# Gathering 64-number node rows instead of 128-number projected rows in a two-layer graph network's message loop

## The reference, cut to what matters

```python
h = jnp.maximum(_layernorm(x, axis=-1), 0.0)          # node rows, 64 numbers
msg_input = jnp.concatenate([h[src], edge_sh, edge_radial], axis=-1)   # 64 + 9 + 8
m = jax.nn.silu(msg_input @ W1 + b1)                  # 81 -> 128
m = jax.nn.silu(m @ W2 + b2)                          # 128 -> 128
messages = m @ W3 + b3                                # 128 -> 64
aggregated = jax.ops.segment_sum(messages, dst, num_segments=6250)
update_input = jnp.concatenate([h, aggregated], axis=-1)
gate = jax.nn.sigmoid(update_input @ G + gb)
u = jax.nn.silu(_layernorm(update_input @ U1 + ub1, ln1_g, ln1_b))
update = _layernorm(u @ U2 + ub2, ln2_g, ln2_b)
out = x + h + gate * update
```

## Time and profile before

| what | value |
|---|---|
| three runs | 3262.56, 3270.5 and 3275.14 us, median 3270.5 |
| span of the profiled execution | 3264.2 us |
| mean granted TensorE clock, as a share of 2.4 GHz | 0.940 |
| busy share PE, DVE, ACT, POOL | 87%, 45%, 47%, 48% |
| data moved | 391.13 MB read, 240.52 MB written |

### The profile page before, as it was taken

One profiled execution on the slowest core, in us unless ns is written; L12 is line 12 of the kernel. 1 busy time (PEld: TensorE's weight loads), 2 busy tenths in 40 slices (PEclk: granted clock), 3 DMA queues, 4 the chain that ended last, 5 costly groups with the idle time before them and its releaser, 6 DMA issues.

```text
span 3264.2 us, 59125 instructions
## 1 busy us (share of the span) xinstructions
PE 2847.1 (87%) x18211; PEld 2118.1 (65%) x18211; DVE 1468.1 (45%) x2016; ACT 1543.7 (47%) x2600; POOL 1565.9 (48%) x1663
## 2 busy tenths in 40 slices
PE   3599999859999969899989888988888989998894
PEld 2477777759989955566555555555555655655563
DVE  7999999863445543222222222222222222222227
ACT  2588888723332214444444444444444444444456
POOL 4000000000000017777777777777777777777765
PEclk8799999959999979999999999999999999999995
DMA  3133333429979966776776777777676777767752
GB/s 127 62 155 157 143 152 157 168 79 370 364 314 352 347 196 181 189 195 189 191 192 189 189 189 194 189 194 189 190 193 189 191 189 190 195 191 191 192 155 68
DMA packets 355148, 632.41 MB, mean 194 GB/s; under 512 B 42566, under 2 KB 251017, under 8 KB 336092
## 3 DMA queue, kind: packets, MB, share of 16 engines
q1 hardware_dynamic: 299973, 519.99, 48.1%
q0 software_dynamic: 54128, 110.18, 15.0%
q10 hardware_dynamic: 1001, 1.66, 0.1%
HBM read 391.13 MB, written 240.52 MB: 194 GB/s over the span
## 4 chain that ended last, share of the span: by engine, by line
PE 37%; POOL 29%; issue 12%; DMA 12%; DVE 8%; ACT 1%; POOLq 0%; DVEq 0%; ACTq 0%
POOL arena L635 27%; PE ps L772 17%; DMA arena<-p_tab,m_idx 11%; PE ps L791 6%; PE ps L949 5%; PE ps L968 3%; DVE arena L1807 2%; PE ps L958 2%; PE ps L946 2%; DVE stageT L1783 2%; POOL arena L648 1%; PE ps L673 1%; PE ps L823 1%; PE ps L661 1%; POOL arena L576 0%
## 5 line engine op out<-in xcount | busy, mean ns | idle before, releaser
L635 POOL DMA_INDIRECT arena<-p_tab,m_idx x1563 | 1474.7, 944 | 1611.2 <-issue 1568.5
L2029 DVE TENSOR_TENSOR_SCAN arena<-arena,ps 128x512 f32<-128x512 f32 x391 | 500.4, 1280 | 1033.8 <-ACT ps L1280 1019.7
L949 PEld LDWEIGHTS ps<-ident,arena 128*128 128x128 f32 x3126 | 391.6, 197 | 517.6 <-DMA arena<-p_tab,m_idx 426.6
L968 PEld LDWEIGHTS ps<-w_fold,arena 128*128 128x128 f32 x3128 | 555.1, 198 | 202.8 <-issue 202.8
L1275 ACT ACTIVATE arena<-ps 128x512 f32<-128x512 f32 x391 | 233.5, 597 | 887.1 <-PE ps L949 884.1
L949 PE MATMUL ps<-ident,arena 128*128 128x128 f32 x3126 | 468.7, 295 | 203.0 <-DMA arena<-p_tab,m_idx 201.7
L968 PE MATMUL ps<-w_fold,arena 128*128 128x192 f32 x3128 | 593.7, 335 | 0.0
L772 PE MATMUL ps<-arena 128*128 128x195 bf16 (+1 forms) x4802 | 481.1, 248 | 31.9 <-DVE arena L1749 31.3
L772 PEld LDWEIGHTS ps<-arena 128*128 128x128 f16 x4802 | 416.5, 98 | 62.8 <-DVE arena L1749 31.5
L946 PE MATMUL ps<-arena,weights 17*128 17x512 f32 x782 | 440.9, 643 | 1.7 <-issue 1.7
L958 PE MATMUL ps<-arena,weights 128*128 128x512 f32 x782 | 427.5, 630 | 0.0
(11 more groups left out here) (257 smaller groups left out, 1637.8 us busy)
## 6 DMA issues: line engine op xcount, KB each, us to landing
arena<-count_d SPq DMA_DIRECT2D x98, 1568.0 KB, 8.6
scan_rows<-arena SPq DMA_DIRECT2D x391, 384.0 KB, 3.5
arena<-keep_d SPq DMA_DIRECT2D x391, 256.0 KB, 4.6
count_d<-arena SPq DMA_DIRECT2D x49, 1568.0 KB, 5.1
arena<-p_tab,m_idx POOLq DMA_INDIRECT x1563
arena<-attr_in SPq DMA_DIRECT2D x391, 34.0 KB
p_tab<-ends SPq DMA_DIRECT2D x12, 256.0 KB, 5.0
wide<-hT_d SPq DMA_DIRECT2D x1, 1617.0 KB
```

The costliest lines, as they stand in the source:

```text
L635: pool.indirect_dma_start(m_rows[:, k, t, :], None, p_tab, bass.IndirectOffsetOnAxis(ap=m_idx[:, k, t:t + 1].bitcast(U32), axis=0))\
L949: last = pe.matmul(x[:, t * P:(t + 1) * P], m_rows[:, k, t, :], ident[:, :], start=False, stop=(t == tiles_of - 1), skip_group_check=True)
L968: last = pe.matmul(m_back[h][:, t * ROW:(t + 1) * ROW], m_scan[:, k % SCAN_RING, e_at:e_at + P], w_fold[:, :], start=True, stop=True)
L2029: dve.tensor_tensor_scan(m_scan[:, k % SCAN_RING, :], m_mask[:, k, :], m_term[k % TERM_RING], before, ALU.mult, ALU.add).then_inc(e1.scan_ ...
```

## The change

**The table.** `p_tab` becomes `m_tab`, which holds the normalised relu'd rows themselves, 64 numbers per node. `multiply_table` and `use_table` go; `stage_table` writes the relu into `hbuf` and SP stores it from there. The turned rows for `hT_d` stay.

**The loop.** POOL gathers 256-byte rows into a ring of 12 slots (`LOOP` 12). PE turns the four tiles (`turn_rows`), ACT copies the turned 64 x 512 next to the 17 attribute rows in SBUF (`keep_turned`), and one product with all 81 rows of W1 follows (`hidden_in`, now one slot behind; W2's product two behind; `LAG` 4). b1 comes in with the first silu. `rows_back` multiplies by W3 alone (64 columns), ACT copies 256 columns in one instruction, and SP stores rows of 64 numbers, four edges next to each other per partition.

**The end.** The gathered 64-number rows are turned (`turn_agg`), copied by ACT (`copy_agg`) and multiplied on PE by the aggregate's rows of U1 and G (`agg_product`), and `add_h` reads that product from PSUM. Groups are six tiles, so there are nine. `turn_update`, `hidden_update` and `update_out` of a group now stand behind the first steps of the next one. `fold` keeps only b3's product.

**The last edges.** Eight more small DVE instructions turn an edge's number into its place in the new layout of `scan_rows`.

```diff
-LOOP = 8
+LOOP = 12
-ROW_RING = MASK_RING = LOOP
-ATTR_RING, TERM_RING, SCAN_RING, OUT_RING = 4, 4, 4, 4
-HID_RING = 2
-LAG = 3
+ROW_RING = LOOP
+MASK_RING = 6
+ATTR_RING, TERM_RING, SCAN_RING, OUT_RING = 4, 3, 4, 4
+HID_RING, BACK_RING = 2, 1
+LAG = 4
...
-END_GROUPS = [(0, 7), (7, 7), (14, 7), (21, 7), (28, 7), (35, 7), (42, 4), (46, 3)]
-GATES_AT = {1: (0, 2), 3: (2, 4), 5: (4, 6), 7: (6, 8)}
+END_GROUPS = [(0, 6), (6, 6), (12, 6), (18, 6), (24, 6), (30, 6), (36, 6), (42, 4), (46, 3)]
+GATES_AT = {1: (0, 2), 3: (2, 4), 5: (4, 6), 7: (6, 8), 8: (8, 9)}
...
-                    pool.indirect_dma_start(m_rows[:, k, t, :], None, p_tab,
+                    pool.indirect_dma_start(m_rows[:, k, t, :], None, m_tab,
...
-                pe.matmul(x, W("W1e"), m_attr[:, k % ATTR_RING, :], start=True, stop=False, skip_group_check=True)
-                pe.wait_ge(e1.gathered[k], DMA * (TB * lap + tiles_of))
-                for t in range(tiles_of):
-                    last = pe.matmul(x[:, t * P:(t + 1) * P], m_rows[:, k, t, :], ident[:, :],
-                                     start=False, stop=(t == tiles_of - 1), skip_group_check=True)
+            def turn_rows(s, k, lap, tiles_of=TB):
+                pe.wait_ge(e1.gathered[k], DMA * (TB * lap + tiles_of))
+                if not isinstance(lap, int) or s >= 1:
+                    pe.wait_ge(e1.turn_kept, s)
+                for t in range(TB):
+                    last = pe.transpose(m_turn[:, t * P:(t + 1) * P], m_rows[:, k, t, :], ident[:, :])
...
+                pe.matmul(m_in, W("W1"), m_msg[:, k % ATTR_RING, :], start=True, stop=True).then_inc(e1.in_done, 1)
...
+                for t in range(TB):
+                    last = pe.matmul(m_back[k % BACK_RING][:, t * D:(t + 1) * D], m_scan[:, k % SCAN_RING, t * P:(t + 1) * P], W("W3"),
+                                     start=True, stop=True)
...
+            def turn_agg(i, a, n):
+                pe.wait_ge(rows_fetched[i], n * DMA)
+                if i >= 1:
+                    pe.wait_ge(agg_copied, i)
+                else:
+                    pe.wait_ge(h_kept, KEEP_UNITS)
...
+            def agg_product(i, n):
+                pe.wait_ge(agg_copied, i + 1)
+                if i >= 1:
+                    pe.wait_ge(u_ready, i)
...
             for i, (a, n) in enumerate(END_GROUPS):
-                turn_update(i, n)
-                update_out(i, n)
+                turn_agg(i, a, n)
+                agg_product(i, n)
+                if i >= 1:
+                    turn_update(i - 1, END_GROUPS[i - 1][1])
+                    update_out(i - 1, END_GROUPS[i - 1][1])
...
             for i, (a, n) in enumerate(END_GROUPS):
+                copy_agg(i, n)
+                if i >= 1:
+                    hidden_update(i - 1, END_GROUPS[i - 1][1])
                 square_u(i, a, n)
                 roots(i, i, i - 2 if i >= 2 else None)
                 if i >= 1:
                     square_v(i - 1, *END_GROUPS[i - 1])
-                hidden_update(i, n)
...
-                dve.wait_ge(rows_fetched[i], n * DMA)
-                dve.tensor_tensor(rows_of, rows_of, of_h[:, a:a + n, :], ALU.add).then_inc(u_ready, 1)
+                dve.wait_ge(agg_multiplied, i + 1)
+                last = dve.tensor_tensor(of_rows[:, a:a + even, :].rearrange("p (b t) f -> p b (t f)", t=2), ps[:, 0:even // 2, 0:2 * ROW],
+                                         of_h[:, a:a + even, :].rearrange("p (b t) f -> p b (t f)", t=2), ALU.add)
```

292 lines of the change are left out of this document (149 added, 143 removed).

## The result

The changed kernel took 3333.3 us (median of four executions, 3308.1 to 3334.9) where the kernel before took 3272.8 us in the same comparison: the ratio is 1.0169, with a 95% interval of 1.0129 to 1.0209. A second comparison on one chip, six executions against 17, gave 3313.7 us (3304.9 to 3328.8) against 3271.2 us: 1.0131, interval 1.0103 to 1.0159. The forecast was 3290 us with a range up to 3310. It had the sign and the lower level of TensorE's clock at the end, and less than half of the size; it took `h_product`, the products of all node rows ahead of the end's groups, as unchanged.

A forecast was written before the change was run, and what follows sets the result against it. POOL's gathers were taken to bound the message loop, with different limits before and behind it. Terms 1.9 - 0.5 - 10.1 - 5.0 + 0 + 3 + 30 = +19.3 us gave 3283.5 us of span, 3290 of time; range 3266 to 3310.

The forecast's parts named there:

- Last edges: Before the layers, at 655 us: eight added small DVE instructions join the chain, 0.24 us each, +1.9 us.
- Table products: First network's last layer: PE's table products go, 37 tiles at 0.272 us, whole gain taken, -10.1 us.
- The last group's way to POOL: Between last layer and loop: scaled group needs only a relu before its store, which starts earlier, -5.0 us.
- the block loads: Rival, last layer: loading of blocks holds PE, so removing table products gains nothing there; 3300 us, chance 0.08.
- The gathers: Message loop: POOL pays per row, not per byte, so 256-byte rows give 0, between -3 and +3 us.
- the cheaper gathers: Rival, message loop: gathers of half the bytes are faster, 10 ns each worth 15.6 us; chance 0.04.
- PE at 1.2 GHz: Rival, message loop: at the low clock PE needs 6.3 us per slot and bounds the loop; near 3,790 us, chance 0.06.
- The tail: After the loop's last gathered rows: longer pipeline and four `rows_back` waiting for one buffer, +3 us, between 1 and 10.
- The end: Groups behind the loop: more work and a longer ring between engines, +17.5 us at 2.4 GHz, +38 at 1.2; +30 taken.
- the ring through DVE and ACT: In the end: copy, product, DVE steps, square and back to the copy set each group's interval, 12.3 or 14.4 us at 1.2 GHz.
- The clock high in the end: Rival, end: PE's clock stays at 2.4 GHz since PE has more to do; sum +6.3, 3277 us, chance 0.22.
- POOL as the bound of the end: Rival, end: handoffs overlap more, so gathers still pace it plus some 5 us latency; 3264 us, chance 0.08.

The follow-up runs named there:

- Experiment 8: Changed kernel with its new table and loop front, but the old fold, 192-number rows and old end put back: median 3260.7 us, ratio 0.9964 to the kernel before.
- experiments 2 and 3: Changed kernel with two PSUM buffers for `rows_back`: median 3301.9 us; then with one buffer and four unused identity turns in each of its three waits: 3307.1 us.
- experiment 4: Changed kernel with ACT's copy of the next group's turned aggregate moved ahead of the square and gates in the end: median 3298.8 us.

## Why the prediction was right or wrong

- *Last edges*, +1.9: right. Eight instructions, 0.22 to 0.24 us apart, add 1.8 us on the chain at 669 us.
- *Table products*, -10.1: the step "the whole gain" failed in size. The gain per body is 0.78 us and not 1.09. This is a body of the last layer in the second execution of the changed kernel, in the chain in order of time:

```profile
1100.65 0.60 PE ps L829 x4
1101.25 4.06 PE ps L768 x49
...
1119.01 0.60 PE ps L829 x4
1119.61 4.04 PE ps L768 x49
```

  It takes 18.36 us, and eight such bodies 18.30 to 18.36, where 18.0 was forecast and 19.10 measured before. In the timeline PE stands 0.24 to 0.29 us ahead of L829, ended by DVE's staging of the table (L1954): with its product gone PE arrives earlier, and the chain of small steps on DVE and ACT that makes the table's rows is what it waits for. It isn't the block loads, the rival that I had named. Over 37 tiles, 9.25 x 0.78 = 7.2 us. With the edges, the fold and the last group (below) that is 1.8 - 0.5 - 7.2 - 3.3 = -9.2 us, against -9.6 by the starts. Experiment 8, which has the levels of before in both stretches, measures table and last group together: -10.4 us, where the two terms forecast -15.1.
- *The last group's way to POOL*, -5.0: measured -3.3. From the end of the last block product to the first gather there were 26.3 us (1176.6 to 1202.9) and now 23.0 (1160.7 to 1183.7). Half a microsecond of the missing 1.7 lies at the start, where DVE comes late to the last block's sums, 0.4 between there and the store, and 0.8 in the store, which became longer. Before:

```profile
1199.02 2.55 DMA p_tab<-ends
```

  and after, with half the bytes, in rows of 256 instead of 512:

```profile
1179.10 3.32 DMA m_tab<-hbuf
```

  It took 3.75 us in the profiled execution and 2.87 to 3.75 in the ten traces that took some 3,300 us or less, against 2.38 and 2.55 in the two with 512-byte rows. I had kept 2.55 for a store whose rows changed; that the length of the rows is the cause is likely and not shown.
- *The gathers*, 0: right, 944 to 947 ns at 256 bytes, as at 512 and 768. The loop is longer by 0.2 to 0.5 us (4.0 in the profiled execution, where each gather took 3 ns more); POOL was held by PE for 9 us of the whole loop in the second execution, 0.3 us at a time. The rival of the cheaper gathers is gone, and so is that of PE at 1.2 GHz: the clock was at 8 tenths all through the loop and no dip held POOL longer than that.
- *The tail*, +3: 3.4 to 3.8, right. But it was laid out for its length only. The sentence "four `rows_back` instead of three, each waiting for the one PSUM buffer to be copied out" names the three gaps that cost 15.4 us in the next stage.
- *The end*, +30: this is where the forecast failed, and in two ways. The first is a term that isn't in the sum: "Starting when `of_h` is kept (3165.3 + 16.1 = 3181.4 us before)" took `h_product` as unchanged, since nobody had edited it. Its clock had changed. It is worth 15.4 us (experiments 2 and 3), and with its start and the way to the restart 16.6 (55.6 less the 39.0 below). The second is the choice between the two levels. At 1.2 GHz the walk forecast 96.4 us for eight intervals and a loss of 38 behind `of_h`; measured are 95.9 us and, from the last pass of `h_product` to the end of the second execution, 121.8 - 82.8 = 39.0. I took 30, on the argument that the clock would come back at times, as in the dip of the earlier trace rows. In the windows of the eight intervals it stood at 0.50 throughout:

```profile
3272.26 0.79 ACT L1372 ACTIVATE arena<-ps 64x768 f32<-64x768 f32 x1
3273.06 1.28 ACT L1380 ACT_TABLE_LOAD   x1
3273.09 4.21 PE L1012 MATMUL ps<-weights,arena 64*128 64x192 f32 x12 [1.06 <-ACT arena L1372]
...
3277.34 1.36 DVE L2080 TENSOR_TENSOR arena<-ps,arena 128x1152 f32<-128x1152 f32 x1 [4.22 <-PE ps L1012]
```

  The pieces of a group are as forecast (copy 0.79 of 0.8, product 4.21 where 3.9 were taken, add 1.36 of 1.36), and DVE's 81.7 us of waiting ahead of `add_h`, 42.8 of them before the first, are all ended by PE. That the sum is so near is in part luck. The forecast had the ring through DVE and ACT at 12.3 us, 14.4 with a gate, and PE's own row at 9.7. The intervals with a gate are that ring (13.6 to 14.1 us, and 11.75 once the copy is moved ahead). Those without one took 11.75 to 11.9 us and kept them in experiment 4, where the copy had left that ring: there PE's row with the waits inside it, which I had left out, is as long.
- *The sum.* Forecast 19.3 us, measured 49.9 with both stretches at the levels of before (40 if the first layer's level belongs to the program). Of the missing 30.6, 16.6 are `h_product`, 9.0 the level taken for the ring, 4.1 the table and the store (9.6 gained instead of 13.7), and 0.9 loop and tail. A further 14 us in the first comparison are the level of the input layer, which by their times was low in three of four executions of the changed kernel. And the 6.3 us that I put around the span are 1.8 (3333.7 against 3331.9, and the same in nearly every execution); the other 4.5 were the distance of the profiled execution from the median.
- *The chances.* The clock high in the end (0.22) and POOL as the bound of the end (0.08) are refuted: POOL had all its rows at 3243 us, and the last `add_h` started at 3313. The range did not allow for a clock that differs in a stretch whose own code nobody touched.

## What to carry to other kernels

Work taken off an engine that waits for another was worth nothing there, and the engine cost time in the next stage: look at what the gaps that it leaves, or the one buffer that it makes do with, do to TensorE's clock right before the next dense stretch. Cost every PE stretch behind an edit at both levels, the unedited ones too, and take a level as given only with a row that shows it under the same gaps. Where two executions of one kernel differ by more than the effect sought, cut the span at a few fixed events and compare part by part.

## What the runs showed of the hardware

- In all three traces with gaps of 0.56 us behind eight passes of 1.08 us each, the clock fell from 2.4 to 1.2 GHz after two or three of them, and 31 us of unbroken passes of 192 columns did not bring it back; in the earlier trace rows it had come back after some 6 us of work. Turns of the identity in the gaps held it (15.8 instead of 31.2 us for the same 98 passes). Why the dense stretch stays low is not known.
- A wait ahead of a stretch doesn't settle its level: 12 passes behind 1.92 us of standing ran at 2.4 GHz (1.55 us), and the 12 behind them, unbroken, at 1.2 GHz (4.21 us).
- The same idle turns gave no time ahead of the node products, and none in the short ring (81.7 for 76.6 us in the profiled executions; 3270.8 for 3268.9 us as the lowest times).
- The clock column reads 1.00 from the start until its first recorded change, while passes took 3.25 us per 14 in place of 1.77.
- The last store of the table, 128 x 4 rows, took 2.9 to 3.75 us at 256 bytes a row (ten traces), and 2.4 to 2.55 us at 512 (two traces).
- In two comparisons the kernels ran 22% (the one before) to 27% (the filled gaps) slower than elsewhere, with waits of ACT that nothing in the program explains.
